# Value products of two attentions with values as weights and probabilities as the moving side, in a one-core decoder kernel

## The reference

```python
q, k, v = x @ Wq + bq, src @ Wk + bk, src @ Wv + bv     # 16 heads of 8
scores = einsum('bhqd,bhkd->bhqk', q, k) / sqrt(8)
attn = softmax(scores, axis=-1)
o = einsum('bhqk,bhkd->bhqd', attn, v)                  # the value product
out = layernorm(x + o.reshape(B, S, 128) @ Wo + bo)
```

## Time and profile before

| | |
|---|---|
| median of three timed runs | 5046.01 us |
| profiled execution, its own time | 5045.63 us |
| its span in the trace | 5043.9 us |
| TensorE busy, of the span | 87% |
| VectorE busy | 69% |
| ScalarE busy | 46% |
| mean granted TensorE clock | 0.938 |

### The profile page before, as it was taken

How to read it: one execution, slowest core, us unless ns; L and a number is a source line. 1 busy time by engine, 2 the same in 40 slices (tenths; PEclk the granted TensorE clock), 3 DMA queues, 4 the chain that set the end, 5 groups by cost and what they waited for, 6 DMA issues and landing times. The chain is left out here.

```text
span 5043.9 us, 147959 instructions
## 1 busy us (share of the span) xinstructions
PE 4368.0 (87%) x54045; PEld 3195.0 (63%) x54086; DVE 3502.5 (69%) x8221; ACT 2334.7 (46%) x4101; POOL 1235.0 (24%) x2155
## 2 busy tenths in 40 slices
PE   6986988999899998698997999899899968829986
PEld 5764666556577887476776666577676434416765
DVE  5887883555477777587883555588787667758985
ACT  3554552222244443365783333355686445505553
POOL 1222331000000000122451000133222234405653
PEclk9997997999999999799997999999999989959998
DMA  2011110000000000111000000000011100020001
GB/s 76 13 30 47 37 33 23 1 0 0 11 2 0 0 0 1 43 42 33 18 17 18 1 0 0 4 14 13 24 32 35 50 7 0 0 53 26 23 18 34
DMA packets 138993, 97.90 MB, mean 19 GB/s; under 512 B 38425, under 2 KB 133153, under 8 KB 138273
## 3 DMA queue, kind: packets, MB, share of 16 engines
q1 hardware_dynamic: 138784, 95.06, 6.4%
HBM read 61.43 MB, written 4.19 MB: 13 GB/s over the span
## 5 line engine op out<-in xcount | busy, mean ns | idle before, releaser
L1338 ACT ACTIVATE L1m_G<-L1m_psY,L1m_B 128x512 f32<-128x512 f32 x256 | 175.9, 687 | 286.5 <-PE L1m_psY L1292 277.7
L1003 DVE TENSOR_TENSOR L0f_SG<-L0f_SG,L0f_psY 128x512 f32<-128x512 f32 x176 | 120.8, 686 | 247.7 <-PE L0f_psY L947 247.4
L1268 PEld LDWEIGHTS L1m_psO<-L1m_W,L1m_G 128*128 128x128 f32 x2048 | 243.8, 192 | 64.5 <-issue 35.9
L986 ACT ACTIVATE L0f_SG<-L0f_psY 128x512 f32<-128x512 f32 x176 | 105.1, 597 | 356.8 <-PE L0f_psY L945 356.8
L1268 PE MATMUL L1m_psO<-L1m_W,L1m_G 128*128 128x128 f32 x2048 | 248.2, 276 | 13.1 <-DVE L1m_ACC L1389 13.1
L1292 PE MATMUL L1m_psY<-L1m_XT,L1m_W 128*128 128x512 f32 x512 | 246.0, 604 | 0.8 <-ACT L1m_XT L1320 0.7
L958 PEld LDWEIGHTS L0f_psO<-L0f_W,L0f_G 128*128 128x128 f32 x1408 | 182.0, 191 | 102.0 <-issue 61.9
L1389 DVE SCALAR_TENSOR_TENSOR L1m_ACC<-L1m_psO,L1m_gate,L1m_ACC 128x128 f32<-128x128 f32 x448 | 126.0, 343 | 163.5 <-PE L1m_psO L1268 161.4
L958 PE MATMUL L0f_psO<-L0f_W,L0f_G 128*128 128x128 f32 x1408 | 188.4, 277 | 17.1 <-DVE L0f_G L1007 10.9
L947 PE MATMUL L0f_psY<-L0f_XT,L0f_W 128*128 128x512 f32 x352 | 180.6, 595 | 2.3 <-issue 0.2
L945 PE MATMUL L0f_psY<-L0f_XT,L0f_W 128*128 128x512 f32 x352 | 181.5, 598 | 0.7 <-ACT L0f_G3T L974 0.7
(11 more groups left out here) (646 smaller groups left out, 12892.1 us busy)
## 6 DMA issues: line engine op xcount, KB each, us to landing
L0a_KB<-L0a_KT SPq DMA_DIRECT2D x128, 32.0 KB, 1.8
stats_rms_chunk<-in_ctx SPq DMA_DIRECT2D x8, 512.0 KB, 4.0
L0x_CS<-in_ctx SPq DMA_DIRECT2D x32, 128.0 KB, 2.2
L0x_CR<-in_ctxT SPq DMA_DIRECT2D x32, 128.0 KB, 2.3
L0x_KB<-L0x_KT SPq DMA_DIRECT2D x128, 32.0 KB, 1.8
L1x_MI<-in_mask SPq DMA_DIRECT2D x32, 128.0 KB, 3.3
L1x_CR<-in_ctxT SPq DMA_DIRECT2D x32, 128.0 KB, 3.0
L1x_KB<-L1x_KT SPq DMA_DIRECT2D x128, 32.0 KB, 1.8
```

The costliest lines, as they stand in the source:

```text
L986: nc.scalar.activation(SG[:, yb, :], psY[:, yb, 0, :], ACT.Silu).then_inc(S["silu"].sem, 1)
L1003: nc.vector.tensor_tensor(SG[:, yb, :], SG[:, yb, :], psY[:, yb, 1, :], ALU.mult).then_inc(S["product"].sem, 1)
L1268: i_ = nc.tensor.matmul(psO[:, ob, j, :], G[:, m % 2, c, j * P:(j + 1) * P], W2[:, m, c, :], start=c == 0, stop=c == fc - 1)
L1338: i_ = nc.scalar.activation(G[:, m % 2, c, :], psY[0:fw, yb, 0, :], ACT.Relu, bias=B1[:, m, c:c + 1])
```

## The change

In L1f and L2x (`late`) the two sides of the value product change places. The weights are now a 128x32 piece of `VB` (18 columns used, padded to 32), the moving side is the 64 columns of `PT`. Four heads' pairs lie side by side in the output's partitions (32 rows each) and four groups of 64 columns follow each other in `psV`, which has the place of the old `psO` in `psB`. Since the queries are now on the free axis, ScalarE copies `psV` to `OV` (128x256), and TensorE turns it back with two 128x128 transposes into `psO`, now a part of `psP`; VectorE reads its sums and products there. New semaphores `ov` (copy done) and `o_rows` (turned back) carry this. The second half of the `PR` transposes now also waits for `normed`, since it writes where the new `psO` lies. The other five attentions keep the old form. The new lines in the changed kernel are L521 (product), L556 (transposes), L593 (copy).

```diff
-            VB = mem.sb("VB", [P, 2, 4, HP, VW])
+            late = 1 if ks is None and not keymask else 0
+            VB = mem.sb("VB", [P, 2, 4, HP, 32 if late else VW])
...
+            OV = mem.sb("OV", [P, 2, 2 * P])
...
-            psO, psOT, psJ = psB[:, 0:HP * VW], psP[:, 0, 0, :], psP[:, 1, 0, :]
+            psV, psOT, psJ, psO = psB[:, 0:2 * P], psP[:, 0, 0, :], psP[:, 1, 0, :], psP[:, 1, 1:3, :] if late else psB[:, 0:HP * VW]
...
                             for hb, freed, read, n, turned in ((0, "pt_a", "ot", A.t - 2 - e, "turned_a"), (1, "pt_b", "res", A.t - 3 - e, "turned_b")):
+                                if hb and late:
+                                    made(pe, "normed", A.t - 1)
                                 made(pe, freed, A.t)
...
-                            made(pe, "normed", A.t)
-                            for b in range(HP):
-                                for s in range(2):
-                                    m = nc.tensor.matmul(psO[64 * s:64 * s + 64, b * VW:(b + 1) * VW], PT[:, A.par, b, 64 * s:64 * s + 64],
-                                                         VB[:, A.u, 2 * A.par + s, b, :], start=True, stop=True)
+                            if late:
+
+                                made(pe, "ov", A.t)
+                                pace(pe, S)
+                                for n in range(4):
+                                    for j in range(4):
+                                        b, s = n // 2 * 4 + j, n % 2
+                                        m = nc.tensor.matmul(psV[32 * j:32 * j + 32, n * SEQ:(n + 1) * SEQ], VB[:, A.u, 2 * A.par + s, b, :],
+                                                             PT[:, A.par, b, 64 * s:64 * s + 64], start=True, stop=True)
...
                             nc.tensor.matmul(psJ, OT[:, A.par, :], o, start=True, stop=True).then_inc(S["proj"].sem, 1)
+                        A = T - 2
+                        if late and A.ok:
+
+                            made(pe, "ov", A.t + 1)
+                            made(pe, "pt_b", reached(T, T.t, TILES))
+                            made(pe, "normed", A.t)
+                            for n in range(2):
+                                m = nc.tensor.transpose(psO[:, n, :], OV[:, A.par, n * P:(n + 1) * P], ident)
+                            m.then_inc(S["o_rows"].sem, 1)
...
                                 nc.scalar.activation(PT[:, A.par, 4 * hb:4 * hb + 4, :], psP[:, hb], ACT.Copy).then_inc(S[done].sem, 1)
+                        A = T - 2
+                        if late and A.ok:
+                            made(act, "pv", A.t + 1)
+                            made(act, "o_rows", A.t - 1)
+                            nc.scalar.activation(OV[:, A.par, :], psV, ACT.Copy).then_inc(S["ov"].sem, 1)
...
-                        o3 = psO.rearrange("p (b c) -> p b c", c=VW)
-                        if A.ok:
-                            made(dv, "pv", A.t + 1)
-                            nc.vector.reciprocal(rden[:, A.par], o3[:, :, 2 * HD:VW]).then_inc(S["recip"].sem, 1)
+                        o3 = psO.rearrange("p g (j c) -> p (g j) c", c=32) if late else psO.rearrange("p (b c) -> p b c", c=VW)
+                        if A.ok:
+                            made(dv, "o_rows" if late else "pv", A.t + 1)
+                            nc.vector.reciprocal(rden[:, A.par], o3[:, :, 2 * HD:2 * HD + 2]).then_inc(S["recip"].sem, 1)
```

More of the change, by code:

```diff
@@ L243, in attention @@
             e = 1 if ln_o else 0
-            late = 1 if ks is None and not keymask else 0
             turn_c = cross and norm is not None
@@ L261, in _ @@
                     nc.vector.memset(VB[0:64, :, :, :, 2 * HD:2 * HD + 1], 1.0)
-                    nc.vector.memset(VB[64:128, :, :, :, 2 * HD + 1:VW], 1.0)
+                    nc.vector.memset(VB[64:128, :, :, :, 2 * HD + 1:2 * HD + 2], 1.0)
                 @block.gpsimd
@@ L510, in slot @@
                             made(pe, "o_v", A.p + 1)
-                            made(pe, "normed", A.t)
-                            for b in range(HP):
-                                for s in range(2):
-                                    m = nc.tensor.matmul(psO[64 * s:64 * s + 64, b * VW:(b + 1) * VW], PT[:, A.par, b, 64 * s:64 * s + 64],
-                                                         VB[:, A.u, 2 * A.par + s, b, :], start=True, stop=True)
+                            if late:
[6 more added lines that the diff above has]
+                                                             PT[:, A.par, b, 64 * s:64 * s + 64], start=True, stop=True)
+                            else:
+                                made(pe, "normed", A.t)
+                                for b in range(HP):
+                                    for s in range(2):
+                                        m = nc.tensor.matmul(psO[64 * s:64 * s + 64, b * VW:(b + 1) * VW], PT[:, A.par, b, 64 * s:64 * s + 64],
+                                                             VB[:, A.u, 2 * A.par + s, b, :], start=True, stop=True)
                             m.then_inc(S["pv"].sem, 1)
@@ L709, in attention @@
             S.advance(dict(scaled=PAIRS), affine is not None)
+            S.advance(dict(ov=TILES, o_rows=TILES), late)
             S.advance(dict(ctx_centred=PAIRS), norm == "ln" and cross)
```

## The result

The changed kernel takes 5104.81 us (median of 4 runs, 5101.68 to 5107.25) against 5046.29 for the kernel before beside it: a ratio of 1.0112, 95% interval 1.0094 to 1.0129. It is slower by 58 us where 45 were forecast. The profiled execution has a span of 5101.1 us against 5043.9, so 57.2 us are to be found in the traces. First the page after: its span and busy times.

A forecast was written before the change was run, and what follows sets the result against it. TensorE was taken to bound both stages, VectorE close; after the change, a ScalarE-TensorE ring of waits. 43.4 us for it plus 1.6 for clearing on 5045.63, and 0.4 against the median, gave 5091 us, range 5076 to 5120.

The forecast's parts named there:

- The ring: L1f and L2x: ScalarE to TensorE to ScalarE waits set the pair at 8.85 us against 8.15, +43.4 us over 62 pairs.
- ScalarE's way behind the product: Even slot: product, `OV` copy, value copies, exponential, `OT`, next L501 follow in sequence, 4.85 us where it was 4.12.
- TensorE's way in the odd slot: Odd slot: transposes wait for the `OV` copy, then scores and projection to L501; 4.00 us, as before, against ScalarE's 3.83.
- The copy's waits: ScalarE idle before the `OV` copy until the product ends: about 0.6 us in even slots, 0.2 in odd.
- The product's length: TensorE's product: four output groups run side by side, 0.47 us instead of 0.93, so 0.47 gained a tile.
- The rival of a product not run side by side: TensorE's product takes 0.93 us, pair 9.79, total 5149 us; chance 10%.
- The hole after L438: TensorE, even slot: idle time where the tile shape changes ahead of the product, +0.09 us.
- the clearance on TensorE: TensorE's own work, shorter product less two added transposes and a hole, falls by 0.41 us a pair if nothing waits.
- The lags of the forecast: Engine-to-engine delays in L1f and L2x, off by 0.1 us a slot or so: 12 us either way, 5079 to 5103.
- Clearing: Zeroing `VB` before each stage grows from 1152 to 2048 columns, +0.79 us each, uncovered: +1.6 us.
- VectorE's cover: Odd slot: VectorE's subtraction ends at 2.05 us, ahead of the exponential at 2.55, leaving 0.5 us to spare.
- the faster rival (5022): L1f and L2x: waits don't close into a ring, TensorE's 0.41 us a pair is gained in full, 5022 us; chance 4%.

The follow-up runs named there:

- the kernels with half a maximum: Row maximum over 32 of 64 keys: in the next-slot-copy kernel with turning before the `ON` transpose, 5039.77 us; in the kernel before, 5039.65 us.
- the two controls: Loops of L1f and L2x begin one slot later: in the kernel before, 5050.42 us; in the kernel with copy and turning one slot later, 5048.27 us.
- the free copy: Changed kernel, but the `OV` copy reads constant data and doesn't wait for the product (results not the attention's): 5054.97 us, ratio 1.0015.

## Why the prediction was right, and where not

**The ring, right.** ScalarE's way behind the product was put at 4.85 us from L504 to L504 in the even slot, and measured at 4.86; TensorE's way in the odd slot at 4.00, and measured at 4.00. The copy's waits were put at 0.6 and 0.2 and are 0.60 and 0.20 in the trace. That these waits are the cause is shown from both sides: without the wait 50 us go away, with a longer step 33 come, and with part of the chain moved ahead of the wait 17 go.

**The product's length, nearly.** The rival of a product not run side by side is out: the group takes 0.65 us, and its 32 records start within 0.43, about 0.014 apart. (That 16 matmuls leave 32 records is what the traces show, not what each record does.) The floor of about 25 ns from start to start in the Trainium skill (TensorE: Matmul & The Clock Gate, "Wait — 56ns, not 53.3ns?"), which would have made it 0.80 as an estimate from that page, does not hold for this product with its four output groups. But from the product's start to the next group it is 0.58, where 0.03 + 0.47 was counted; it was 0.99 before, so a tile gains 0.41, where 0.47 was put. The hole after L438 is about 0.1, as forecast. So the clearance on TensorE was mis-sized: 0.41 a pair forecast; the kernels with half a maximum put it at 0.22 (8.04 less 7.82), as far as TensorE holds them both.

**The missing term.** The forecast took a pair as the unit and 31 pairs a stage, and never asked where the loop's jump lies. In an odd slot TensorE's way is the longer one, so a hole in it is paid for: +0.4 to 0.5 us, 11 times a stage, 11 us. That the jump's place costs this is shown by moving the jump (13 us back) and by the two controls that gave nothing. Why the hole is there stays open. The expectations took it that a jump is bare only where TensorE's last instruction ahead of it has just waited; the free copy and the half maximum speak against that, since there the hole stands with no such wait. What the traces have in common is the time since the slot's last release: at a jump the scores start 0.83 to 0.89 us behind the end of the `OV` copy in every version whose copy and turning stand in one slot (0.42 without a jump in the changed kernel), and 1.15 to 1.20 behind the second `PT` copy in the two with the turning ahead of the `ON` transpose (down to 0.82 without a jump). That TensorE's program can run ahead only from such a release on, and then has the jump in its way, is my reading; no run varies it alone. The Trainium skill (Advanced Engine Details and Errata, "Control Flow Timing") has about 108 ns for a compare and branch; the hole here is 0.4 larger than the 0.37 without a jump, several times that figure, so the branch alone would not explain it.

**The range, by luck.** The lags of the forecast gave 5079 to 5103, and 5104.81 lies outside that. It lies inside 5076 to 5120 only because the range was widened for the product that is not run side by side, which did not happen: the room kept for that rival took up the jumps, a cost that was never counted.

**The rest.** Clearing was put at +1.6 and is +1.5. VectorE's cover was enough in the changed kernel, as said: its waits grew. But its room was thought larger than it is. With the copy's wait out of the way the stage lands at 8.07 a pair, no better than before. So the faster rival (5022) was wrong twice over: the ring closes, and where it is kept open VectorE is next at once, with the jump close behind: with the turning earlier, easing VectorE brings the mean from 8.09 to 8.00 only, and 0.185 of that is the jump. What makes 8.07 out of VectorE's 7.36 stays open: the one named wait that I took out left the mean where it was.

## What to carry to other kernels

On an engine that works in order, an evacuation that waits for a product of its own slot delays all that is queued behind it, and the price is read off the ring, not off the copy's length: put it one slot later, behind work that is due anyway (here that took the whole 58 us away). A shorter matmul group pays only as far as the next engine has room; here VectorE was about 0.1 us a pair behind TensorE, and no placing of the copy beat the kernel before. Count in the unit in which the code repeats, the four slots of the loop, and look whether its jump falls in a slot that the jumping engine bounds.

## What the runs showed of the hardware

Four column groups of 128x32 run side by side if their matmuls alternate: 32 records in 0.65 us, against 1.39 for the same ones group by group, where two groups overlap only in part. Where TensorE's program jumps back ahead of the scores, they start 0.36 (0.56 for 0.20, half a maximum) to 0.44 us (0.75 for 0.31, free copy) later than elsewhere, and where TensorE bounds the slot it is 0.37 (4.12 for 3.75) to 0.55 us (4.55 for 4.00) longer. In the kernel before, L535 to L462 is mostly 0.36 in L1f and 0.32 in L2x at its jumps, and 0.32 elsewhere, and moving the jump changed nothing that can be measured.
